# Adding the experts' rows to a table of the tokens by accumulating scatters

## The reference

```
def _fuse_moe(x, ln_g, ln_b, rw, rb, fc1_w, fc1_b, fc2_w, fc2_b):
    h = _ln(x, ln_g, ln_b)
    logits = h @ rw.T + rb
    vals, idx = jax.lax.top_k(logits, K)            # K = 2 of 8 experts
    gates = jax.nn.softmax(vals, axis=-1)
    N = x.shape[0] * x.shape[1]
    hf = h.reshape(N, D)
    h1 = jax.nn.gelu(jnp.einsum('nd,efd->enf', hf, fc1_w) + fc1_b[:, None, :], approximate=False)
    eo = jnp.einsum('enf,edf->end', h1, fc2_w) + fc2_b[:, None, :]
    ...
    gathered = eo[idx_f, jnp.arange(N)[:, None], :]
    mixed = (gathered * gates_f[..., None]).sum(axis=1).reshape(x.shape)
    return x + mixed
```

## Time and profile before

| | us |
|---|---|
| median of three runs | 1943.75 |
| profiled execution | 1940.73 |
| its span in the trace | 1939.2 |
| MOE, from the first scatter to the landing of the last | 1748.30 to 1917.90 |
| from there to the end of the span | 21.3 |

### The profile page before, as it was taken

How to read it: one execution, slowest core, us unless ns; L and a number is a source line. 1 busy time by engine, 2 the same in 40 slices (tenths; PEclk the granted TensorE clock), 3 DMA queues, 4 the chain that set the end, 5 groups by cost and what they waited for, 6 DMA issues and landing times. The chain is left out here.

```text
span 1939.2 us, 54781 instructions
## 1 busy us (share of the span) xinstructions
PE 1621.0 (84%) x17114; PEld 1295.5 (67%) x17114; DVE 1329.5 (69%) x4084; ACT 1199.0 (62%) x3451; POOL 946.9 (49%) x1389
## 2 busy tenths in 40 slices
PE   6999999999996869999999775479998884448981
PEld 5888888888884747667777662157776664437771
DVE  3777777777775638888777536668887883337772
ACT  2776777677674426677777335468888771137771
POOL 3354344444441454556665434534454444646773
PEclk8999999999998979999999787579999995559996
DMA  9676666766662022221000000000000000136765
GB/s 240 150 155 139 157 148 137 162 141 151 149 146 58 1 92 107 94 105 43 19 18 11 1 1 1 0 4 1 0 10 13 12 9 23 44 110 213 215 212 155
DMA packets 214819, 167.06 MB, mean 86 GB/s; under 512 B 27632, under 2 KB 188784, under 8 KB 214448
## 3 DMA queue, kind: packets, MB, share of 16 engines
q1 hardware_dynamic: 206128, 142.75, 29.1%
q0 software_dynamic: 8576, 22.88, 3.6%
HBM read 91.79 MB, written 73.76 MB: 85 GB/s over the span
## 5 line engine op out<-in xcount | busy, mean ns | idle before, releaser
L738 ACT ACTIVATE sb_probs<-sb_probs,sb_work 128x128 f32<-128x128 f32 x512 | 198.6, 406 | 120.3 <-DVE sb_work L641 120.3
L281 POOL TENSOR_SCALAR sb_next_var_eps<-sb_next_moments 128x1 f32<-128x1 f32 (+1 forms) x184 | 45.3, 246 | 433.2 <-DVE sb_next_moments L721 246.6
L890 POOL TENSOR_TENSOR sb_work<-sb_work,sb_cols 128x512 f32<-128x512 f32 x128 | 134.2, 1048 | 215.6 <-ACT sb_work L1107 133.6
L1033 DVE TENSOR_REDUCE sb_work<-PS 128x8 f32<-128x512 f32 x256 | 175.3, 685 | 46.9 <-PE PS L932 44.5
L1035 DVE TENSOR_TENSOR sb_work<-PS,sb_work 128x512 f32<-128x512 f32 x256 | 177.1, 692 | 8.8
L1067 ACT ACTIVATE sb_work<-sb_work 128x512 f32<-128x512 f32 x256 | 161.6, 631 | 33.4 <-DVE sb_work L1035 27.5
L906 PE MATMUL PS<-sb_ident,sb_work 128*128 128x128 f32 x1024 | 150.0, 287 | 15.9 <-ACT sb_work L1107 10.6
L959 PEld LDWEIGHTS PS<-sb_v_ones,sb_work 128*64 128x64 f32 x4096 | 133.0, 140 | 24.7 <-issue 16.9
L959 PE MATMUL PS<-sb_v_ones,sb_work 128*64 128x18 f32 x4096 | 144.9, 214 | 4.6 <-ACT sb_work L1073 2.8
L1073 ACT ACTIVATE sb_work<-PS 128x512 f32<-128x512 f32 x256 | 139.7, 594 | 10.1 <-PE PS L906 6.8
L906 PEld LDWEIGHTS PS<-sb_ident,sb_work 128*128 128x128 f32 x1024 | 113.8, 145 | 43.5 <-issue 31.3
(11 more groups left out here) (281 smaller groups left out, 4467.1 us busy)
## 6 DMA issues: line engine op xcount, KB each, us to landing
rel_scratch<-sb_work SPq DMA_DIRECT2D x64, 516.0 KB, 7.3
sb_work<-rel_scratch SPq DMA_DIRECT2D x64, 512.0 KB, 6.6
expert_rows<-sb_blank SPq DMA_DIRECT2D x36, 520.0 KB, 2.9
sb_w_up<-expert_halves SPq DMA_DIRECT2D x23, 512.0 KB, 3.6
sb_w_down<-expert_halves SPq DMA_DIRECT2D x23, 512.0 KB, 3.4
expert_halves<-sb_e_halves POOLq DMA_DIRECT2D x16, 512.0 KB, 6.2
sb_work<-expert_rows SPq DMA_DIRECT2D x23, 260.0 KB, 3.3
sb_e_raw<-e_W POOLq DMA_DIRECT2D x16, 256.0 KB, 5.3
```

What stands on the lines that cost most here:

```text
L738: ins = e.activation(probs[:, j], probs[:, j], ACT.Exp, bias=neg_max[:, j:j + 1], scale=-1.0, accum_out=row_sum[:, j:j + 1])
L890: e.tensor_tensor(k_masked[:, u3], k_sb[:, u3].rearrange("p (b k) -> p b k", b=2).unsqueeze(2) .to_broadcast([P, 2, 4, S]), col("place").u ...
L1033: e.tensor_reduce(top, mine, AX.X, ALU.max).then_inc(sem("att_max_ready"), 1)
```

## The change

The table in the memory becomes one of tokens: 4096 rows, and 512 spare ones. In the phase ROUTE, SP stores X into it (and zeros into the spare rows) by five DMAs. The scatters of MOE go to the row of the token, whichever of its two choices the row is, and carry `compute_op=ALU.add`: the DMA adds the row to what stands there. Before the first scatter POOL also waits for the five stores. After the last scatter SP copies the table to the output, memory to memory, by four DMAs. The eight loads, DVE's eight additions and the four stores of X are gone. The table `ids` holds each token's number twice in place of 8192 different numbers.

```
+        token_sums = nc.dram_tensor("token_sums", [NTOK + GROUP, D], F32, kind="Internal").ap()
-        expert_outs = nc.dram_tensor("expert_outs", [2 * NTOK + GROUP, D], F32, kind="Internal").ap()
...
+        def route_sync(e, c):
+            for j in range(4):
+                e.dma_start(token_sums[0:NTOK].rearrange("(t p) d -> p t d", p=P)[:, NT // 4 * j:NT // 4 * (j + 1)],
+                            X[:, NT // 4 * j:NT // 4 * (j + 1)]).then_inc(sem("tokens_out"), 16)
+            e.dma_start(token_sums[NTOK:].rearrange("(t p) d -> p t d", p=P), blank[:, :, 0:D]).then_inc(sem("tokens_out"), 16)
...  (moe_sync)
             e.wait_ge(sem("moe_returned"), 16 * QT * NG)
-            e.wait_ge(sem("moe_down_done"), NG)
+            whole = out.rearrange("b s d -> (b s) d")
             for j in range(4):
-                for i in range(2):
-                    e.dma_start(returned(i, j), expert_outs[bass.ds(i * NTOK + j * NTOK // 4, NTOK // 4)]
-                                .rearrange("(t p) d -> p t d", p=P)).then_inc(sem(f"moe_rows_loaded{j}"), 16)
-            for j in range(4):
-                e.wait_ge(sem("moe_mixed"), 2 * j + 2)
-                e.dma_start(out.rearrange("(t b) s d -> (b s) t d", b=2)[:, NT // 4 * j:NT // 4 * (j + 1)],
-                            X[:, NT // 4 * j:NT // 4 * (j + 1)]).then_inc(sem("out_written"), 16)
+                r = slice(j * NTOK // 4, (j + 1) * NTOK // 4)
+                e.dma_start(whole[r].rearrange("(p t) d -> p (t d)", p=P), token_sums[r].rearrange("(p t) d -> p (t d)", p=P))\
+                    .then_inc(sem("out_written"), 16)
...  (moe_vector)
-            for j in range(4):
-                e.wait_ge(sem(f"moe_rows_loaded{j}"), 16 * ((NG - j + 3) // 4) + 32)
-                xs = X[:, NT // 4 * j:NT // 4 * (j + 1)]
-                for i in range(2):
-                    wait(e, sem("moe_mixed"), 2 * j + i)
-                    e.tensor_tensor(xs, xs, returned(i, j), ALU.add).then_inc(sem("moe_mixed"), 1)
...  (moe_pool)
                     wait_alone(e, sem("moe_returned"), 16 * QT * g)
+                    if g == 0:
+                        wait_alone(e, sem("tokens_out"), 16 * 5)
                     for t in range(QT):
                         e.indirect_dma_start(
-                            out=expert_outs, out_offset=bass.IndirectOffsetOnAxis(
+                            out=token_sums, out_offset=bass.IndirectOffsetOnAxis(
                                 ap=rows_in[:, g % RB, t, D:D + 1].bitcast(U32), axis=0),
-                            in_=y_rows[:, g % 2, t], in_offset=None).then_inc(sem("moe_returned"), 16)
+                            in_=y_rows[:, g % 2, t], in_offset=None, compute_op=ALU.add).then_inc(sem("moe_returned"), 16)
...  (lay_out, on the host)
-    T["ids"] = c(np.arange(2 * NB * S + QT * P, dtype=np.uint32).reshape(-1, P).T)
+    n = np.arange(NB * S + QT * P, dtype=np.uint32)
+    T["ids"] = c(np.concatenate([n[:NB * S], n]).reshape(-1, P).T)
```

More of the change, by code:

```diff
@@ L1716, in build @@
         h_hi, h_lo = h_parts
-        def returned(i, j):
-            return h_parts[i][:, j // 2, 2 * (j % 2):2 * (j % 2) + 2].bitcast(F32)\
-                .rearrange("p a (t d) -> p (a t) d", d=D)
         def moe_sync(e, c):
@@ L1863, in build @@
         L2 = dict(gpsimd=l2_pool, tensor=l2_tensor, vector=l2_vector, scalar=l2_scalar)
-        ROUTE = dict(gpsimd=route_pool, tensor=route_tensor, vector=route_vector, scalar=route_scalar)
+        ROUTE = dict(sync=route_sync, gpsimd=route_pool, tensor=route_tensor, vector=route_vector, scalar=route_scalar)
         MOE = dict(sync=moe_sync, gpsimd=moe_pool, tensor=moe_tensor, vector=moe_vector, scalar=moe_scalar)
```

## The result

The changed kernel takes 2002.33 us (median; 1999.62 to 2004.91), the one before, on the same chip, 1945.90 us: a ratio of 1.0294 with a 95% interval of 1.0271 to 1.0317. It is slower by 56.4 us. The forecast was +13.4, with a range up to 2000: the direction was right, the size a quarter of what came, and the range was missed by 2 us.

A forecast was written before the change was run, and what follows sets the result against it. POOL was taken to pace MOE, waiting for each group's landing. Landings 16.1 plus issue on POOL 9.2 less 11.9 saved at the end gave +13.4 us, 1957.1 us; range 1932 to 2000.

The forecast's parts named there:

- The pace of MOE: In MOE's loop, POOL sets the pace at 7.51 us a group, and any longer landing goes into every group at full length.
- The end: Behind the last landing: one wait, four issues and the copy take 9.4 us in place of 21.3, saving 11.9.
- The stores in ROUTE at nothing: In ROUTE, the five new stores take 8.0 us but are hidden in SP's wait of 110.2 us, so cost nothing.
- The landing, d = 0.7: Added landing time of an adding scatter, 0.7 us, on the path 23 times: 16.1 us; by the ends 0 and 33.8.
- The issue, e = 0.10: Added time on POOL for each adding scatter, 0.10 us, 92 times: 9.2 us; by the ends 0 and 44.2.
- The estimate of 0.15: Alternative added landing time of an adding scatter, in us, worked out from the Trainium skill's statements.
- The free add: Rival for MOE's scatters: landing 0.22 us longer, nothing added on POOL; -6.8 us, 1937.0 us; chance 0.28.
- Descriptors decide: Rival on POOL's issue: each adding scatter takes 0.48 us more, landing as forecast; +48.4 us, 1992.2 us; chance 0.13.
- The low clock: Rival in MOE: TensorE falls to 1.2 GHz and PE paces at 12.7 us a group; 2031 us; chance 0.07.
- The copy: Rival at the end: memory to memory runs at half rate, saving only 4.8 us; +20.5, 1964 us; chance 0.05.

The follow-up runs named there:

- the experiment by rows: Kernel before, with single plain and adding DMAs from POOL behind its last store; the add costs POOL 0.62, 0.50 and 0.46 us at 128, 64 and 32 rows.
- the small weight loads: Changed kernel with the experts' weight loads from the third group on cut to a sixteenth; 1983.47 us against 1937.13 of the kernel before, ratio 1.0228.
- two semaphores: Kernel before with landings of even and odd groups counted separately, so POOL need not wait for the group just ahead, except in the last three; 1928.58 us against 1937.13.

## Why the prediction was right or wrong

**The pace of MOE** was read rightly: PE starts 0.10 us behind POOL's `x_lo` in both kernels but for the first groups, ACT's rows are ready before the landing, so landings are on the path, and taking the wait off it gained 8.6 us.

**The end** was sized rightly: 9.4 us forecast, 8.97 measured; the run without the add shows it alone. The DMA engines are busy for 0.68 of it, 6.1 us, where the sum had 7.1 for the bytes. (The prediction's first paragraph has nothing but DMAs at work in the end of before; the earlier trace rows have DVE busy for 9.80 us there, as its part on the end says.)

**The stores in ROUTE at nothing** holds: SP waited 110.2 us there and waits 109.9, ROUTE's scatters take as long with the stores as without them, and without the add the loop is as before.

**The landing, d = 0.7.** In the quiet groups it is 4.00 - 2.95 - 0.60 = 0.45, in the loop, where the weights are loaded beside it, 4.76 - 3.45 - 0.59 = 0.72: 20 x 0.72 + 3 x 0.45 = 15.8 us against 16.1 forecast. The size is right, and in part by luck: 0.27 of the 0.72 come only beside the weight loads, which the prediction's d did not have, and the half that it took of a small load's 1.47 us rested on no row that splits a load. The fetch of the row in memory was to cost it; what the traces show is that the DMA engines work four times as long on one-row packets, longer still on more bytes, and that the landing is later beside the weights. How much of it is the fetch was not shown. The estimate of 0.15 that the prediction works out from the Trainium skill ("DMA: Bandwidth & Descriptors", Anatomy of one DMA, and "Collectives: The Full Stack", The bandwidth ceiling) holds in neither place; the measurement decides.

**The issue, e = 0.10, is the step that failed.** "... a descriptor at an address already known should cost less than that. I take 0.10." It is 0.58: the mean of the 92 rows is 1.633 us against 1.049 (the medians, 1.557 and 0.972, differ by as much), so 92 x 0.584 = 53.7 us where the sum had 9.2. Even the upper end, half of a scatter's 0.96, was below it. Both were made from a model, cost by descriptor, and the experiment by rows shows that most of it does not depend on the rows. The trace of before could not show that; but an operation that it does not show at all has no upper end in a share of another operation. With the measured terms the sum is 53.7 + 15.8 - 12.3 = +57.2, beside +56.4 of the medians.

**The rivals.** The free add is refuted by both terms. "Descriptors decide" came nearest in size, +48.4, and with it the lesson that POOL's issue counts 92 times, but not the reason. The low clock came in part: 0.88 was granted in the loop, between the two levels, where the prediction looked for 1.00. It did not set the pace: the product kept starting behind `x_lo`, a group took 10.67 us and not the 12.7 of a PE at 0.50, and with the small weight loads the loop got faster at a clock as low. The copy ran at 234 GB/s and saved what it should.

**The chances.** 0.56 on slower was right; the 0.13 on a cost at the issue was too little for a term with no row behind it and a factor of 92.

## What to carry to other kernels

Count what an edit adds to every instruction of the engine that paces a loop before looking at what it saves behind the loop: 12 us at the end were paid for with 0.58 us in each of 92 scatters. An operation that the trace does not show, times a large count, deserves a probe or a wide range, not a share of its nearest relative. And a wait for the landing of the DMAs just ahead on the pacing engine is worth looking for: two semaphores gave back 8.6 us, where this change was to save 11.9.

## What the runs showed of the hardware that was not expected

- An adding scatter occupies POOL for 0.45 to 0.46 us longer than a plain one at 32 rows and 0.56 to 0.62 at 128, with rows of 512 B as with rows of 2 KB; a direct adding DMA for 0.3 us longer than a plain one.
- It moves one row of 512 B per packet (144 packets for a scatter of 128 rows, 32 for the plain one), and the DMA engines are busy 0.7 us with it in place of 0.18; with rows of 2 KB, in as many packets, 2.0 us in place of 0.7.
- Beside weight loads at a DMA share of 0.67, such scatters land 0.7 us later than alone; plain ones 0.5.
- Copying 2.10 MB from memory to memory in rows of 32 KB took 8.97 us from the last landing to the end, at 234 GB/s over that stretch.
